# Lengths of keys and queries in the front of a gated delta layer: sums of squares as rows over four column tiles

## The reference, cut to what matters

```
def _l2norm(x, eps=1e-06):
    return x * jax.lax.rsqrt(jnp.sum(x * x, axis=-1, keepdims=True) + eps)
...
qkv = jax.nn.silu(_causal_conv1d(qkv, conv_weight))
...
q = _l2norm(q) * Dk ** (-0.5)
k = _l2norm(k)
...
decay_mask = jnp.exp(jnp.clip(g[..., :, None] - g[..., None, :], -30.0, 30.0))
attn = -(jnp.einsum('bhcid,bhcjd->bhcij', k_beta, k) * decay_mask)
```

## Time and profile before

| what | us |
|---|---|
| median of three timed runs | 4169.28 |
| lowest and highest of them | 4161.04, 4176.44 |
| the profiled execution, device time | 4157.96 |
| its span from the first to the last instruction | 4156.2 |
| stage d_front in it, 1296 to 1806 | 510.00 |
| in that stage busy: PE, DVE | 474.78, 433.99 |
| in that stage busy: ACT, POOL | 323.58, 217.79 |

### The profile page before, as it was taken

The page is one execution under the profiler, slowest core; times in us unless marked ns, Lnnn a source line. Parts: engine busy times, 40 slices in busy tenths (PEclk is TensorE's granted clock), DMA queues, the critical chain, the costliest instruction groups (busy, mean ns, idle before and its releaser), DMA issues. The chain is left out here.

```text
span 4156.2 us, 73250 instructions
## 1 busy us (share of the span) xinstructions
PE 3794.4 (91%) x25346; PEld 2785.3 (67%) x25346; DVE 2563.9 (62%) x6909; ACT 2176.8 (52%) x5705; POOL 943.5 (23%) x849
## 2 busy tenths in 40 slices
PE   7989988888985999979999999999999999979778
PEld 4555555555553666658888888888888888855344
DVE  4752468887335899856666666666666666532632
ACT  3741267776114666646666666665666666622222
POOL 0010000000001435342333323233233233221211
PEclk9999999999996999989999999999999999979879
DMA  2010100000004666543333333333333333222002
GB/s 80 2 35 0 50 1 2 2 2 16 20 1 129 211 219 207 219 137 92 97 74 92 80 90 91 82 94 97 81 95 83 86 90 81 61 86 80 20 29 92
DMA packets 443148, 322.82 MB, mean 78 GB/s; under 512 B 330208, under 2 KB 380064, under 8 KB 440736
## 3 DMA queue, kind: packets, MB, share of 16 engines
q1 hardware_dynamic: 439712, 309.75, 26.0%
q0 software_dynamic: 3072, 8.39, 0.6%
HBM read 200.13 MB, written 117.88 MB: 77 GB/s over the span
## 5 line engine op out<-in xcount | busy, mean ns | idle before, releaser
L2453 ACT ACTIVATE d_heads_VP<-d_heads_chain,d_GALL 128x128 f32<-128x128 f32 x512 | 189.0, 369 | 632.6 <-PE d_heads_chain L2347 629.2
L2596 DVE SCALAR_TENSOR_TENSOR d_heads_S<-d_heads_S,d_GALL,d_heads_chain 128x128 f32<-128x128 f32 x768 | 232.7, 344 | 381.3 <-PE d_heads_chain L2354 379.3
L2532 POOL TENSOR_TENSOR d_heads_KD<-d_heads_KR,d_GALL 128x512 f32<-128x512 f32 x256 | 270.0, 1075 | 284.2 <-ACT d_heads_KR L2421 284.2
L637 ACT ACTIVATE b_heads_PR<-b_heads_sc,b_heads_NM 128x128 f32<-128x128 f32 (+3 forms) x512 | 269.3, 534 | 114.8 <-DVE b_heads_NM L701 114.5
L2233 PE MATMUL d_heads_value<-all_XT,d_heads_WVZ 128*128 128x256 f32 x1024 | 292.6, 389 | 19.2 <-POOL d_heads_ZS L2511 19.2
L2378 PE MATMUL d_heads_projected<-d_heads_WO,d_heads_OT 128*128 128x256 f32 x1024 | 288.4, 395 | 20.2 <-ACT d_heads_OT L2472 20.2
L2020 DVE SCALAR_TENSOR_TENSOR d_front_CY<-d_front_proj,d_CW,d_front_CY 128x511 f32<-128x511 f32 (+2 forms) x384 | 271.9, 744 | 49.9 <-ACT d_front_CY L1931 45.4
L2574 DVE SCALAR_TENSOR_TENSOR d_heads_CY<-d_heads_value,d_CW,d_heads_CY 128x511 f32<-128x511 f32 (+2 forms) x384 | 283.1, 741 | 22.1 <-ACT d_heads_CY L2414 22.0
L2255 PE MATMUL d_heads_value<-d_heads_WVZ,all_XT 128*128 128x256 f32 x1024 | 284.6, 380 | 1.3 <-DVE d_heads_CY L2574 1.3
L2354 PEld LDWEIGHTS d_heads_chain<-d_heads_VP,d_heads_KD 128*128 128x128 f32 x1792 | 262.9, 191 | 31.0 <-ACT d_heads_VP L2453 9.5
L2354 PE MATMUL d_heads_chain<-d_heads_VP,d_heads_KD 128*128 128x128 f32 x1792 | 277.2, 277 | 5.9 <-ACT d_heads_VP L2453 5.9
(11 more groups left out here) (348 smaller groups left out, 8908.6 us busy)
## 6 DMA issues: line engine op xcount, KB each, us to landing
d_kq<-d_front_KQ SPq DMA_DIRECT2D x64, 768.0 KB, 4.6
d_heads_KQ<-d_kq SPq DMA_DIRECT2D x64, 768.0 KB, 4.9
d_heads_GE<-d_gerows SPq DMA_DIRECT2D x128, 256.0 KB, 5.3
d_front_GR<-d_grows SPq DMA_DIRECT2D x32, 512.0 KB, 6.5
d_it<-d_front_LI SPq DMA_DIRECT2D x64, 256.0 KB, 2.1
d_l<-d_front_LI SPq DMA_DIRECT2D x64, 256.0 KB, 3.7
d_heads_ITB<-d_it SPq DMA_DIRECT2D x128, 128.0 KB, 2.8
d_heads_WVZ<-w_d_qkvz SPq DMA_DIRECT2D x32, 256.0 KB, 6.5
```

Of the source, the lines that this page charges most:

```text
L637: nc.scalar.activation(PR[p % 3][j][:, at:at + w], SC[p % 2][j][:, at:at + w], ACT.Exp, bias=NM[:, u % 2, t, slot:slot + 1], scale=-1.0 if ...
L2532: nc.gpsimd.tensor_tensor(KD[i % 2][:, 4 * q:4 * q + 4, h, :], KR[q][:, :, :], decay, ALU.mult).then_inc(kds, 1)
L2596: stt(S[:, h, :], S[:, h, :], gate(i, GEL0 + h, c), R[h][:, HD:2 * HD], ALU.mult, ALU.add).then_inc(su, 1)
```

## The change

The sums of squares are now made in two steps. First four calls (`square_rows`, L1902 of the changed kernel) take a 128x32 block of ones as weights and two chunks of squares each (256 columns) as data. Each call writes 32 partitions of d_front_ssq, so that the lengths lie along rows, each repeated 32 times; the four calls use the four column tiles of the array. ACT copies these rows into d_front_RW (`copy_rows`, L1955), 128x256. Then `lengths` (L1912) turns them into columns: two calls with 128 columns of d_front_RW as weights and four columns of the identity as data. All of it belongs to the visit before: PE runs projection of i + 1, rows of i - 1, products of i, lengths of i - 1. On DVE `norms` of a group moves to b = 0 of the next, on POOL `exponents` come first and `scale` and `root` of the group before follow, and SP stores d_l one visit later. The scratch of the inverse (TMP) is now a slice of XN.

The diff, without the lines that only pass XN on and name semaphores:

```
-        ones = s.sb("ones", [P, 1])
+        ones = s.sb("ones", [P, HB])
...
+        RW = [s.sb(f"RW{r}", [P, 2, P]) for r in range(2)]
...
-        INV, TO, TMP = s.sb("INV", [P, HB, HB]), s.sb("TO", [P, HB, HB]), s.sb("TMP", [P, HB * HB // 4])
+        INV, TO, TMP = s.sb("INV", [P, HB, HB]), s.sb("TO", [P, HB, HB]), XN[:, 0, :]
...
-                if b == 1 and g >= 1:
+                if b == 2 and g >= 1:
                     store_l(g - 1)
...
+            def square_rows(i):
+                pe.wait_ge(squares, i + 1)
+                if i >= 1:
+                    pe.wait_ge(rowc, i)
+                if i % BATCH == 0 and i > 0:
+                    pe.wait_ge(kss, i)
+                for q in range(4):
+                    mm = nc.tensor.matmul(SSQ[q * HB:(q + 1) * HB, 0:2 * P], ones[:, :],
+                                          SQ[i % 2][:, 2 * q:2 * q + 2, :, :].rearrange("p c k n -> p (c k n)"),
+                                          start=True, stop=True)
+                mm.then_inc(srow, 1)
+
             def lengths(i):
                 g, b = divmod(i, BATCH)
-                pe.wait_ge(squares, i + 1)
-                if b == 0 and g >= 1:
-                    pe.wait_ge(kss, 4 * g)
-                for c in range(NCH):
-                    at = (g % 2) * 32 + b * NCH + c
-                    mm = nc.tensor.matmul(SSQ[:, at:at + 1], SQ[i % 2][:, c, :, :].rearrange("p k n -> p (k n)"),
-                                          ones[:, :], start=True, stop=True)
+                pe.wait_ge(rowc, i + 1)
+                for m in range(2):
+                    at = 2 * P + (g % 2) * 32 + b * NCH + m
+                    mm = nc.tensor.matmul(SSQ[:, at:at + NCH - 1:2], RW[i % 2][:, m, :], C.ident[:, 0:P:HB],
+                                          start=True, stop=True)
                 mm.then_inc(ssq, 1)
...
                     project_keys(i + 1)
+                if i >= 1:
+                    square_rows(i - 1)
                 products(i)
-                lengths(i)
+                if i >= 1:
+                    lengths(i - 1)
+            square_rows(VISITS - 1)
+            lengths(VISITS - 1)
...
+            def copy_rows(i):
+                act.wait_ge(srow, i + 1)
+                if i >= 2:
+                    act.wait_ge(ssq, i - 1)
+                nc.scalar.copy(RW[i % 2][:, :, :], SSQ[:, 0:2 * P].rearrange("p (m n) -> p m n", m=2)).then_inc(rowc, 1)
...
                     tap(i + 1)
+                if i >= 1:
+                    copy_rows(i - 1)
                 act.wait_ge(silus, 2 * i + 2)
                 if i >= 2:
-                    act.wait_ge(ssq, i - 1)
+                    act.wait_ge(srow, i - 1)
...
             for g in range(HK):
+                if g + 1 < HK:
+                    exponents(g + 1)
                 if g >= 1:
                     scale(g - 1)
-                if g + 1 < HK:
-                    exponents(g + 1)
+                    root(g - 1)
...
-                root(g)
             scale(HK - 1)
+            root(HK - 1)
...
-                if b == 3:
-                    norms(g)
+                if b == 0 and g >= 1:
+                    norms(g - 1)
...
+            norms(HK - 1)
```

More of the change, by code:

```diff
@@ L1781, in invert_step, with delta_front @@
     return nc.vector.tensor_tensor(rest, rest, prod, ALU.add)
-def delta_front(nc, name, XT, GALL, GB, CW, grows, kq_d, it_d, l_d, uq_d, tq_d, W, C):
+def delta_front(nc, name, XN, XT, GALL, GB, CW, grows, kq_d, it_d, l_d, uq_d, tq_d, W, C):
     with Stage(nc, name) as s:
@@ L1809, in delta_front @@
         gr = [s.sem(f"rows{r}") for r in range(2)]
-        (const, filled, args, clips, exps, proj, taps, convstep, convs, silus, squares, ssq, kkq, lis, kss, rinvs, rn2,
+        (const, filled, args, clips, exps, proj, taps, convstep, convs, silus, squares, srow, rowc, ssq, kkq, lis, kss, rinvs, rn2,
          nbs, lsc, invl, diag, inv, turned, ust) = (s.sem(n) for n in (
-             "consts", "filled", "args", "clips", "exps", "proj", "taps", "convstep", "convs", "silus", "squares", "ssq",
+             "consts", "filled", "args", "clips", "exps", "proj", "taps", "convstep", "convs", "silus", "squares", "square_rows",
+             "rows_copied", "ssq",
              "kkq", "lis", "kss", "rinvs", "rn2", "nbs", "lscaled", "inv_loaded", "diagonal", "inverse", "inverse_turned",
@@ L1964, in _ @@
                     nc.scalar.copy(TO[:, :, :], INV[:, :, :].rearrange("p a n -> p n a")).then_inc(turned, 1)
+            copy_rows(VISITS - 1)
         @blk.gpsimd
@@ L2046, in norms @@
                     dve.wait_ge(lsc, BATCH * (g - 1))
-                two = lambda lo: SSQ[lo:lo + CHUNK, (g % 2) * 32:(g % 2) * 32 + 32].rearrange("p (b c) -> p b c", b=BATCH)
+                two = lambda lo: SSQ[lo:lo + CHUNK, 2 * P + (g % 2) * 32:2 * P + (g % 2) * 32 + 32].rearrange("p (b c) -> p b c", b=BATCH)
                 for lo in (0, CHUNK):
@@ L2653, in delta_net @@
                 delta_gates(nc, "d_gates", BA, W, C, GALL, GB, CW, grows, gerows)
-            delta_front(nc, "d_front", XT, GALL, GB, CW, grows, kq_d, it_d, l_d, uq_d, tq_d, W, C)
+            delta_front(nc, "d_front", XN, XT, GALL, GB, CW, grows, kq_d, it_d, l_d, uq_d, tq_d, W, C)
         delta_heads(nc, "d_heads", X, XT, GALL, CW, gerows, kq_d, it_d, l_d, uq_d, tq_d, W, C)
```

## The result

| | before | after |
|---|---|---|
| median of five timed runs, us | 4167.18 | 4139.93 |
| lowest and highest of them | 4160.75, 4176.44 | 4136.97, 4144.00 |
| the profiled execution | 4157.96 | 4142.65 |
| stage d_front in it, first memset on GpSimd to that of the next stage | 511.36 | 490.30 |

The ratio is 0.9936, with a 95% interval of 0.9919 to 0.9954: 27 us faster, against a forecast of 4144 and 25. That rest is the same code in every run of this document; in the thirteen profiled executions it lasts 3644.8 (before, the shortest) to 3655.8 us of the span, 3650.6 in the one of after. So the 6 is spread. What follows is read from the stage.

A forecast was written before the change was run, and what follows sets the result against it. PE was taken to set the front stage's pace (29.17 of 29.85 us a group), DVE close behind. Terms 14.1 + 1.7 + 2.8 + 4 + 2.5 = 25.1 us turned the median 4169.28 into 4144, range 4130 to 4173.

The forecast's parts named there:

- What bounds the kernel: Front stage before the change: PE sets the pace, busy 29.17 of 29.85 us a group, DVE close behind with steps.
- 7.21 us a visit without a pause: PE before the change: projection 3.52, products 1.88 and lengths 1.81 us run without waiting in three of four visits.
- TensorE's terms: PE's visit after the change: 7.21 - 1.81 + 0.45 + 0.74 = 6.59 us, four visits 26.4.
- one after another: Upper bound and rival on PE: column tiles take turns, a visit is 7.91 us, time about 4197; chance 0.10.
- The pace after: DVE and ACT set groups without steps: block 0 6.87, block 1 6.60, blocks 2 and 3 14.03, together 27.50 us.
- With steps: Eight groups with inverse steps on DVE: steps collide with POOL in blocks 3 and 0; 236.0 against 238.82, 2.8 us less.
- the 0.66 taken off for smaller steps: Groups with inverse steps: the largest-step group's 30.13 us less 0.66 makes the mean group 29.5.
- Root: POOL's root moves behind the scaling, over blocks 1 and 2, without cost; rival: it locks DVE, 66 us, chance 0.04.
- Start and end: First visits and end of the front stage: 4 us less at the start, 2.5 less at the end.
- Sum: All terms of the front stage: 14.1 + 1.7 + 2.8 + 4 + 2.5 = 25.1 us less, time 4144.
- The likeliest case: The forecast itself, for the whole kernel: 21 to 36 us less, chance 0.50.
- the largest term: The six groups without steps between first and last group: 2.35 us less each, 14.1 us.

The follow-up runs named there:

- full width: The changed kernel with rows made by a 128x128 block of ones instead of four 128x32 tiles, most lengths left out; 4179.83 us, ratio 1.0028.
- norms first: The changed kernel with the norms ahead of the two decayed products in block 0; 4149.86 us, ratio 0.9963 to the kernel before.
- no lengths: The changed kernel with rows, copy and lengths only for the first two groups, later groups reusing those lengths; 4135.83 us, ratio 0.9917.
- both: The changed kernel with inverse steps, then norms, directly behind the convolution and ahead of the decayed products; 4138.67 us, ratio 0.9933.
- the changed kernel again: The changed kernel, unaltered, run once more on the chip of a later run for direct comparison; 4138.03 us, ratio 0.9933.
- GpSimd's order alone: The kernel before with only GpSimd's new order (exponents, scaling, root) and stores of l one visit later; 4174.08 us, ratio 1.0017.
- steps first: The changed kernel with the two inverse steps directly behind the convolution, ahead of decayed products and norms; 4139.97 us, ratio 0.9928.
- loads spread: The changed kernel ordered convolution, steps, norms, decayed products, with SP's sixteen loads for the inverse spread over four visits; 4135.00 us, ratio 0.9923.
- a late square: As loads spread, with square, rows and copy of the visit ahead of the exponential moved behind the next visit's taps; 4129.31 us, ratio 0.9910.

## Why the prediction was right, and which of its terms were off

- *What bounds the kernel.* "7.21 us a visit without a pause" is the step that failed, though the forecast held. It held a wait of 0.20 for the square, and the loop was a ring: square, lengths, projection, tap, square. So 0.73 of a group's gain comes from making the lengths one visit late, and 1.1 from tiles and shorter lengths; the prediction put all of it on the latter.
- *TensorE's terms.* A visit is 6.43 where 6.59 was forecast. The bound "one after another" is out twice: by the 0.64, and by what full width costs. The Trainium skill, "TensorEngine Tiling (Array Packing)", section "Key Properties", says that different tiles can execute weight loads and matmuls in parallel; 0.64 against 1.89 agrees.
- *The pace after.* Blocks 1 and 2 are 6.60 as forecast, block 0 6.98 instead of 6.87, block 3 7.83 instead of 7.43: 28.0, not 27.50. Block 3's 0.39 is the wait of the rows for the norms (gone with norms first). The prediction saw the norms move into block 0 but not that the next rows on TensorE wait for them; their wait was in the diff. With block 0's 0.11 that is 0.5 a group, 3.0 of the 5.4 missing. The rest is the second group, still marked by the start (29.2, and so again in no lengths and in both), one group with the silu's wait of 1.01 for a store (29.0) and one behind products at half clock (28.6). The last two are not the kernel's own: in the changed kernel again they take 28.09 and 28.00.
- *With steps.* Each collision came where it was forecast. The group of the largest steps takes 30.00 where 30.13 was forecast. What failed is the 0.66 taken off for smaller steps: the first of the eight, with the smallest steps, takes 30.52 (30.00 in the changed kernel again), so the mean is 29.7 and not 29.5. Even a step of 128x30 takes 1.03 beside the scaling. The gain is 1.1 (1.7 in the changed kernel again) instead of 2.8; how much of the difference is half-clock products, no run separates.
- *Root.* It held nothing, as the earlier trace rows promised and against the rule of the Trainium skill's "SBUF — State Buffer", "Who interferes with whom", that two SBUF inputs on VectorE contend with a GpSimd instruction that reads SBUF. Beside exponents and scaling the trace agrees with the rule: 1.10 and 1.03 for the steps shown.
- *Start and end.* 6.3 and 3.0 against 4 and 2.5. The start was bounded by one stall alone; the visits behind it were faster too. But not all of the 6.3 is shown to be the change's. With GpSimd's order alone and TensorE's list as before, the start takes 27.36 instead of 30.71, since the clock is up sooner: the projection in question first before, then there (clock 1.00 instead of 0.60).

```profile
1321.93 6.03 PE L1889 MATMUL d_front_proj<-all_XT,d_front_WKQ 128*128 128x512 f32 x8
```

```profile
1320.99 3.68 PE L1889 MATMUL d_front_proj<-all_XT,d_front_WKQ 128*128 128x512 f32 x8
```

  So up to 3.35 of it can be the moment at which the clock rises; no run separates the two. At the end the products ran at full clock.
- *Sum.* 25.1 was predicted, the stage shows 21.4, the medians 27. The six between stage and medians are within the spread of the rest of the program, 11 us over the executions, and no run here says more. The likeliest case was right, with the largest term two fifths too large, and start and end too small by 2.8. That errors of both signs and the spread bring 27 so near to 25.1 is luck; that the groups, the start and the end gain is not.

## What to carry to other kernels

An engine that is busy all the time may still wait in every turn: compare the starts of its instructions with the end of what they wait for, weight loads too, before calling it the bound. When work moves to another place, list what waits for it there and what it releases; here the moved norms made the next rows wait, and norms moved once more released GpSimd into VectorE's steps. What the experiments found on the way (steps first, norms first, loads spread, a late square), all in one kernel, was worth another 13 us in the stage (488.4 to 475.1).

## What was unexpected of the hardware

- The granted clock falls in the middle of the stage, and the length of the pause ahead does not tell when. After the 2.13 us above it was 0.54 and the products took 3.65; after the pauses of 1.13 it stayed at 1.00. The eight groups with steps of after each have a pause of 1.98 or 1.99 ahead of products: four times they then take 2.49 to 3.54, four times 2.05, as in two neighbours:

```profile
1457.42 3.54 PE L1923 MATMUL d_front_kk<-d_front_KQ 128*128 128x128 f32 x16 [1.98 <-ACT d_front_KQ L1974]
...
1486.90 2.05 PE L1923 MATMUL d_front_kk<-d_front_KQ 128*128 128x128 f32 x16 [1.98 <-ACT d_front_KQ L1974]
```

  With GpSimd's order alone the clock falls behind a pause of 0.63, with which the kernel before keeps 1.00 (the window of the projection has 0.68):

```profile
1376.78 2.05 PE L1911 MATMUL d_front_kk<-d_front_KQ 128*128 128x128 f32 x16 [0.63 <-ACT d_front_KQ L1951]
...
1380.68 5.38 PE L1889 MATMUL d_front_proj<-all_XT,d_front_WKQ 128*128 128x512 f32 x8
```

  What sets the moment stays open. In no lengths, where TensorE has least to do, ten of sixteen pauses of 2.01 to 3.25 are followed by slow products (2.66 to 3.54), and six, of up to 2.97, by 2.05.
- A power of 128x32 that occupies GpSimd for 5.43 us in the profile does not hold VectorE's instructions with two SBUF inputs; 128x512 differences and products of 1.0 us each hold even a 128x32 instruction, 0.19 to 1.06.
